# Delta rule levels: one 128x128 block-diagonal tile per matrix instead of two 64x64 tiles, and openings that leave out the next weights

## The chip, the cores and the metric

The kernel runs on one core of one Trainium2 chip. The metric is the time of one execution on the device in microseconds (us).

## The reference, cut to what matters

The program is a transformer of four layers, each an attention part and a feed-forward part, over 8 x 512 rows of 128 numbers in float32. Two of its eight stages hold a delta rule: the attention of layer 0 (here "L0") and that of layer 2 ("L2", with a decay).

```python
A = jnp.where(tri, 0.0, -jnp.einsum('bhncd,bhned->bhnce', kb, k))
for i in range(1, chunk):
    upd = jnp.einsum('...k,...kj->...j', A[..., i, :], A[..., :, :i])
    A = A.at[..., i, :i].add(upd)
inv = A + jnp.eye(chunk, dtype=A.dtype)
u = inv @ v
w = inv @ kb
```

So for each chunk and head a unit triangular matrix is inverted, and its inverse is multiplied with values and keys. The recurrence of L2 is written step by step in the reference; the kernel computes it in chunks as well, with decays in the matrix.

## The kernel before, in words

**Stages and lanes.** The eight stages run one after the other. At each start all compute engines meet: `Run.meet` lets an engine wait for every semaphore that has counted so far. Then the sync engine (SP) issues the DMA that brings the weights of the next stage into the other of two side buffers. A stage's opening clears its buffers on VectorE, the engines meet once more (`run.meet_all()`), and then eight batches are worked off in two lanes, even batches in lane 0 and odd ones in lane 1. Each lane's work is cut into phases, and each engine's instructions are issued in the same order: a phase of lane 0, a phase of lane 1, and so on. An engine works in that order and waits where a semaphore isn't there yet.

**The inverse.** A sequence of 512 steps is four chunks of 128, with four heads. Two chunks are taken together (a pair), which gives 8 matrices of 128x128 (`NT`, the transposed strict part). Each is inverted from its diagonal outwards. First, in level 0, VectorE inverts 2x2 blocks with a few element-wise operations on the four diagonal 32x32 blocks of each matrix (partitions 0 to 31 hold block 0, partitions 32 to 63 block 1, and so on: `part`, `xt` and `x` are 128 x 8 x 32). Levels 1 to 4 join blocks to 4, 8, 16 and 32. Each has a left product (the strict part times the inverse so far, `b[2]`), a mask on VectorE (L899), a right product (L809) with tiles of 32x32, a subtraction (L906) and a 32x32 transpose (L909). Two larger joins follow (L817 to L848), and then the two chunks are applied (L935 and the lines 1089 to 1101 in L0, 2663 to 2675 in L2).

**The left product before.** `strict` is a tile of 128 x 8 x 64. In each half of 64 partitions it holds, for each matrix, a 64x64 tile with two 32x32 blocks on its diagonal; its other half is cleared once at the opening (L791). ScalarE fills it with four copies of 32 partitions (`strict_act`, L856). TensorE multiplies each half with the 64 partitions of `x` in it (L801), so 16 products of 64x64 by 64x32 for each level. VectorE, in `level0_dve`, adds the two 32-column halves of `strict` (L885) to get the diagonal blocks side by side in `part`, masks them (L887), subtracts them from the identity (L889) and transposes (L891).

**Around it.** In L0, TensorE issues after each phase of the first pair a group of six products of a long filter (L1243), and VectorE parts of a short filter (L1258, L1261). In L2, VectorE makes `NT` from the scores and the decays `gt` (L2882), then `AT` (L2885); in L0 ScalarE copies `NT` (L1179) and VectorE masks `AT` (L1316). GpSimd has only the inverse square roots of the norms in these stages (L402, L2948).

Of the kernel before, what the change touches and what calls it, by code (L numbers as in the profile page):

```python
# [7 lines left out]
ALU = mybir.AluOpType  # L8
# [139 lines left out]
                                                  for e in ("PE", "ACT", "DVE", "POOL"))  # L148


class Run:


# [19 lines left out]

    def meet(self, engine):

        for s in self.steps.values():
            if s.count:
                engine.wait_ge(s.sem, s.count)

    def meet_all(self):  # L180
# [571 lines left out]
class Delta:  # L752
# [5 lines left out]
    def __init__(self, c, arena, dv, scaled):  # L758
        self.c, self.dv, self.width = c, dv, HEADS * dv
        self.NT, self.AT, self.X, self.XT, self.T1 = (arena.take(2, HEADS, P) for _ in range(5))  # L760
        small, whole = INVERTED * SMALL, lambda v: v.rearrange("p c h n -> p (c h n)")
        blocks = lambda v, n: v.rearrange("p (m n) -> p m n", n=n)
        self.xt_columns, self.x_columns = whole(self.X)[:, 0:small], whole(self.X)[:, small:2 * small]
        self.xt, self.x = blocks(self.xt_columns, SMALL), blocks(self.x_columns, SMALL)
        self.strict = arena.take(INVERTED, 2 * SMALL)
        self.strict_half = [self.strict[:, :, n * SMALL:(n + 1) * SMALL] for n in range(2)]
        self.part = blocks(whole(self.T1)[:, 0:small], SMALL)
        self.x_half, self.part_half = (blocks(whole(v)[:, 2 * small:], 2 * SMALL) for v in (self.X, self.T1))
        self.NT8, self.XT8 = (v.rearrange("p c h n -> p (c h) n") for v in (self.NT, self.XT))
        self.U = [arena.take(HEADS, dv) for _ in range(2)]  # L770
        self.S, self.gain = arena.take(HEADS * dv), arena.take(HEADS * dv)
        self.own = c(f"blocks{dv}")
        self.carried = arena.take(2, HEADS, dv) if scaled else None
        self.left = self.carried[:, 0] if scaled else arena.take(HEADS, dv)
# [13 lines left out]
    def start_dve(self, dve, u):  # L788

        dve.memset(self.XT, 0.0).then_inc(*u.dve.step())  # L790
        dve.memset(self.strict, 0.0).then_inc(*u.dve.step("strict_cleared"))  # L791

    def levels_pe(self, pe, u, pair, between):
        b = u.banks
        for n in range(1, SMALL_LEVELS):
            pe.wait_ge(*u.dve.at(f"x{pair}_{n - 1}"))
            if n == 1:
                pe.wait_ge(*u.act.at(f"strict{pair}"))
            for m in range(INVERTED):
                for g in map(half_of, range(2)):  # L800
                    made = pe.matmul(b[2][g, m * SMALL:(m + 1) * SMALL], self.strict[g, m, :], self.x[g, m, :])  # L801
            made.then_inc(*u.pe.step(f"left{pair}_{n}"))
            next(between, None)
            yield f"left{pair}_{n}"
            pe.wait_ge(*u.dve.at(f"part{pair}_{n}"))
            half = SMALL // 2
            for m in range(INVERTED):
                for q in map(quarter, range(QUARTERS)):
                    made = pe.matmul(packed(b[3][q, m * half:(m + 1) * half], n), self.part[q, m, :],  # L809
                                     odd_blocks(self.xt[q, m, :], n))  # L810
            made.then_inc(*u.pe.step(f"right{pair}_{n}"))
            next(between, None)
            yield f"right{pair}_{n}"
# [39 lines left out]
    def strict_act(self, act, u, pair):  # L853

        for i in range(QUARTERS):
            act.copy(self.strict_half[i % 2][quarter(i)], self.NT8[quarter(i), :, quarter(i)]).then_inc(*u.act.step(f"strict{pair}"))  # L856

    def levels_act(self, act, u, pair):
        b, half = u.banks, 2 * SMALL
# [22 lines left out]

    def level0_dve(self, dve, u, pair):
        dve.wait_ge(*u.act.at(f"strict{pair}"))
        dve.tensor_tensor(self.part, *self.strict_half, ALU.add).then_inc(*u.dve.step())  # L885
        dve.wait_ge(*u.dve.last())
        dve.tensor_tensor(self.part, self.part, per_tile(self.c("small0"), INVERTED), ALU.mult).then_inc(*u.dve.step())  # L887
        dve.wait_ge(*u.dve.last())
        dve.tensor_tensor(self.xt, per_tile(self.c("small_ident"), INVERTED), self.part, ALU.subtract).then_inc(*u.dve.step())  # L889
# [87 lines left out]
class L0AttnLane:  # L977
    def __init__(self, c, arena, vT, shortT, vearly, vrow):
        self.norm, self.delta = Norm(arena), Delta(c, arena, DK, False)
        self.vT, self.shortT, self.longT = vT, shortT, arena.take(SEQ)  # L980
        self.vearly, self.vrow, self.lrow = vearly, vrow, vearly
        self.before = {name: arena.take(L0_ATTN_CONV - 1 + SEQ) for name in "qkv"}
        self.stat_rows = arena.take(TILES, HEADS, 32)
        self.z, self.zT = arena.take(TILES, P), arena.take(SEQ)
        self.qrow, self.krow, self.vb, self.kb, self.drow, self.kT = (arena.take(TILES, P) for _ in range(6))
# [14 lines left out]
class L0Attn:  # L1000
# [417 lines left out]
    def pool(self, pool, u):  # L1418
# [3 lines left out]
        for phase in ("features", "project", "convolve", "rows", "norms", "keys"):  # L1422
            yield phase
        for pair in range(CHUNKS // 2):
            yield from delta_phases(pair)
        for phase in ["branches", "squares", "lengths", "statistics", "gate", "hidden", "logits", "softmax", "mix",
                      "out", "end"]:
# [1131 lines left out]
class L2AttnLane:  # L2559
    def __init__(self, c, arena):  # L2560
# [5 lines left out]
        self.kbq = arena.take(TILES, 2, P)  # L2566
        self.gt, self.gtm = arena.take(2, HEADS, P), arena.take(2, HEADS, P)
        self.conv = [all_heads(v) for v in (self.gt[:, 0], self.gt[:, 1], self.gtm[:, 0], self.gtm[:, 1])]
        self.steps = [self.a, self.delta.T1[:, 0]]
        self.beta, self.g, self.log = (arena.take(TILES, HEADS) for _ in range(3))  # L2570
        self.low, self.one_more, self.rest = (arena.take(TILES, HEADS) for _ in range(3))
# [8 lines left out]
class L2Attn:  # L2580
# [360 lines left out]
    def pool(self, pool, u):  # L2941
# [10 lines left out]
            yield phase  # L2952
        for pair in range(CHUNKS // 2):
            yield f"between{pair}"
            yield from delta_phases(pair)
        yield "squares"
        yield "roots"
# [916 lines left out]
```

## Time and profile before

| what | value |
|---|---|
| time, median of 3 runs | 5654.37 us (5648.27 to 5659.23) |
| profiled execution, its own time | 5665.99 us |
| its span | 5664.6 us |
| instructions | 93833 |
| TensorE matmul busy | 4062.2 us, 72% |
| TensorE weight load busy | 3146.2 us, 56% |
| VectorE busy | 3020.7 us, 53% |
| ScalarE busy | 1912.0 us, 34% |
| GpSimd busy | 818.4 us, 14% |
| mean granted TensorE clock | 0.76 |

PE is the matmul part of TensorE, PEld its weight loads, DVE is VectorE, ACT is ScalarE, POOL is GpSimd, SPq the queue of SyncE. The granted clock is given as a share of 2.4 GHz: 0.50 is 1.2 GHz. A float32 matmul leaves two records, and so does its weight load; a transpose leaves one. The L0 stage lies between about 17 and 990 us of the span, the L2 stage between about 2844 and 3810 us.

### The profile page before, as it was taken

The page shows a single profiled execution, that of the slowest core. Times are in us where ns is not written, and L with a number is a line of the kernel's source. Part 1 is how long each engine was busy: PE and PEld are TensorE (multiplying, and loading weights), DVE is VectorE, ACT ScalarE, POOL GpSimd, SP SyncE. Part 2 cuts the span into 40 slices and gives each one's busy share as a digit, 9 for nine tenths or more (in the row PEclk, how much of TensorE's full clock was granted, in tenths as well). Part 3 has the DMA queues.
Part 4 walks back from the last instruction along what each step waited for, and adds up shares of the span by engine and source line. Part 5 has one row for each costly group of instructions (what it writes and reads, how often), then busy time and mean ns, then how long its engine had stood idle before and what let it go on. Part 6 is the DMA issues. An engine that isn't in the chain of part 4 may idle for free.

```text
span 5664.6 us, 93833 instructions
## 1 busy us (share of the span) xinstructions
PE 4062.2 (72%) x39179; PEld 3146.2 (56%) x39228; DVE 3020.7 (53%) x8021; ACT 1912.0 (34%) x4196; POOL 818.4 (14%) x600
## 2 busy tenths in 40 slices
PE   6685967568878778773757768577777777776398
PEld 5574846446556555562646557464444555445377
DVE  4445364234554555547255665657666666665333
ACT  2234232123333333330232332325444455552122
POOL 0000000321011101101700000001222111110444
PEclk6555555677898898885756666668888998897599
DMA  9200000330000000001210000000000000000255
GB/s 266 54 2 1 2 1 1 105 113 1 1 1 1 1 1 1 1 1 37 31 41 1 1 1 2 1 2 1 1 1 1 1 1 1 1 1 17 72 164 141
DMA packets 140856, 152.26 MB, mean 27 GB/s; under 512 B 7809, under 2 KB 128003, under 8 KB 139793
## 3 DMA queue, kind: packets, MB, share of 16 engines
q1 hardware_dynamic: 119024, 128.21, 7.7%
q0 software_dynamic: 21408, 18.05, 1.9%
q8 instruction: 309, 5.06, 0.4%
q14 instruction: 115, 0.93, 0.1%
HBM read 87.38 MB, written 59.76 MB: 26 GB/s over the span
## 4 chain that ended last, share of the span: by engine, by line
PE 50%; DVE 29%; ACT 13%; issue 3%; POOL 3%; DMA 2%; SPq 0%; DVEq 0%; POOLq 0%; ACTq 0%
ACT work L3242 4%; PE banks_lane L801 4%; PE banks_lane L422 3%; PE banks_lane L3679 2%; PE banks_lane L1882 2%; PE banks_lane L809 2%; PE banks_lane L3128 2%; PE banks_lane L935 2%; PE banks_lane L3163 1%; ACT work L1976 1%; PE banks_lane L3108 1%; PE banks_lane L3150 1%; POOL room_l_ffn L569 1%; DVE work L2797 1%; DVE weights L3252 1%
## 5 line engine op out<-in xcount | busy, mean ns | idle before, releaser
L422 PE MATMUL banks_lane<-constants,work 128*128 128x128 f32 x968 | 194.4, 346 | 456.2 <-DVE work L408 209.2
L422 PEld LDWEIGHTS banks_lane<-constants,work 128*128 128x128 f32 x968 | 145.3, 178 | 524.9 <-DVE work L408 196.9
L422 PE MATMUL banks_lane<-constants,weights 128*128 128x128 f32 x596 | 126.2, 349 | 349.8 <-DVE weights L408 94.9
L402 POOL TENSOR_TENSOR weights<-weights,constants 128x4 f32<-128x4 f32 x76 | 78.6, 1034 | 1929.6 <-DVE weights L397 1929.6
L422 PEld LDWEIGHTS banks_lane<-constants,weights 128*128 128x128 f32 x596 | 89.3, 180 | 381.6 <-issue 175.0
L3242 ACT ACTIVATE work<-banks_lane,weights 128x192 f32<-128x192 f32 (+1 forms) x512 | 249.3, 505 | 132.5 <-DVE weights L3339 132.5
L402 POOL TENSOR_TENSOR work<-work,constants 128x4 f32<-128x4 f32 x76 | 77.5, 1019 | 1208.8 <-DVE work L397 1208.8
L3346 POOL TENSOR_TENSOR weights<-weights,constants 128x16 f32<-128x16 f32 x64 | 185.5, 2898 | 377.3 <-DVE weights L3254 377.3
L3335 DVE TENSOR_REDUCE weights<-banks_lane 128x2 f32<-128x384 f32 (+1 forms) x256 | 122.4, 520 | 140.2 <-PE banks_lane L3150 140.2
L2029 DVE TENSOR_REDUCE work<-banks_lane 128x2 f32<-128x512 f32 x256 | 158.8, 683 | 67.7 <-PE banks_lane L1896 67.2
L3163 PE MATMUL banks_lane<-constants,work 128*128 128x128 f32 x896 | 135.5, 297 | 80.7 <-DVE work L3327 42.2
L1976 ACT ACTIVATE work<-banks_lane 128x384 f32<-128x384 f32 (+1 forms) x256 | 118.5, 549 | 178.2 <-PE banks_lane L1917 110.0
L3163 PEld LDWEIGHTS banks_lane<-constants,work 128*128 128x128 f32 x896 | 108.1, 152 | 104.5 <-issue 57.0
L3679 PE MATMUL banks_lane<-weights,work 128*128 128x256 f32 x624 | 145.1, 386 | 14.5 <-DVE weights L3721 14.5
L3178 PE MATMUL banks_lane<-work 128*64 128x128 f32 x1792 | 128.1, 288 | 37.2 <-ACT work L3204 37.2
L656 POOL DMA_INDIRECT out<-weights,chunk_places x78 | 121.5, 1558 | 196.5 <-DVE chunk_places L648 130.3
L569 POOL DMA_INDIRECT room_l_ffn<-weights,indices x96 | 92.8, 966 | 362.1 <-DVE weights L392 324.7
L1882 PE MATMUL banks_lane<-weights,work 128*128 128x128 f32 x1024 | 136.7, 298 | 5.9 <-ACT work L1998 5.9
L1882 PEld LDWEIGHTS banks_lane<-weights,work 128*128 128x128 f32 x1024 | 132.7, 213 | 10.3 <-ACT work L1998 10.3
L801 PE MATMUL banks_lane<-work 64*64 64x32 f32 x2048 | 125.1, 292 | 16.5 <-DVE work L891 13.0
L3679 PEld LDWEIGHTS banks_lane<-weights,work 128*128 128x128 f32 x624 | 116.9, 192 | 34.0 <-DVE weights L3721 19.3
L3178 PEld LDWEIGHTS banks_lane<-work 128*64 128x64 f32 x1792 | 100.7, 142 | 62.2 <-ACT work L3204 49.6
(773 smaller groups left out, 10869.7 us busy)
## 6 DMA issues: line engine op xcount, KB each, us to landing
work<-experts_dram_l_ffn SPq DMA_DIRECT2D x39, 964.0 KB, 4.9
room_l_ffn<-work SPq DMA_DIRECT2D x30, 1188.0 KB, 14.7
work<-experts_dram_l_ffn SPq DMA_DIRECT2D x23, 512.0 KB, 3.6
weights<-weights_dram SPq DMA_DIRECT2D x1, 4833.5 KB, 14.3
work<-room_l_ffn SPq DMA_DIRECT2D x36, 132.0 KB, 4.0
weights<-weights_dram SPq DMA_DIRECT2D x1, 4112.0 KB, 13.1
weights<-bands_dram SPq DMA_DIRECT2D x1, 4096.0 KB, 13.1
weights<-room_l_ffn SPq DMA_DIRECT2D x26, 132.0 KB, 4.3
```

The lines of the kernel that those rows point to most:

```text
L402: pool.tensor_tensor(n.rstd, n.rstd, c("neghalf", cols=(0, n.rstd.shape[1])), ALU.pow).then_inc(*u.pool.step(name))
L422: done = pe.transpose(bank[0:rows, t * P:(t + 1) * P], block, c("ident"))
L569: pool.indirect_dma_start(self.room, bass.IndirectOffsetOnAxis(ap=self.where[:, n, t:t + 1], axis=0), rows[n][:, t, :], None).then_inc(*se ...
L801: made = pe.matmul(b[2][g, m * SMALL:(m + 1) * SMALL], self.strict[g, m, :], self.x[g, m, :])
L1882: made = pe.matmul(b[1][:, cols_of(t)], m.ff[:, f, cols_of(t)], self.w(u, f"down{f}"), start=f == 0, stop=f == L1_ATTN_FF - 1)
L1976: act.activation(m.probs[:, hh, 0:blocks, :].rearrange("p b q -> p (b q)"), b[hh][:, 0:blocks * P], ACT.Exp, scale=L1_ATTN_SCALE).then_inc ...
L2029: dve.tensor_reduce(m.top[r][:, :, hh, L1_ATTN_HD], b[hh][:, :].rearrange("p (t c) -> p t c", t=2), AX, ALU.max, negate=True).then_inc(*u. ...
L3163: made = pe.transpose(u.banks[2 + side][:, cols_of(hh)], m.probs[n % 2][:, hh, side * P:(side + 1) * P], self.c("ident"))
L3178: made = pe.matmul(u.banks[2][rows, cols_of(j)], m.v[:, t - 1 + side, at:at + L2_FFN_HD], m.turned[n % 2][:, 4 * side + hh, :], start=side ...
L3242: act.activation(m.probs[n % 2][:, hh, L2_FFN_BACK + lo:2 * P], u.banks[side][:, j * span:(j + 1) * span], ACT.Exp, scale=m.q_factor[:, t, ...
L3346: pool.tensor_tensor(m.rn[:, t, :, :], m.rn[:, t, :, :], c("neghalf", cols=(0, 2 * L2_FFN_HEADS)).rearrange("p (n h) -> p n h", n=2), ALU. ...
L3679: made = pe.matmul(bank[:, g * CHUNK:(g + 1) * CHUNK], self.w(u, f"{name}{f}", cols=(g * P, (g + 1) * P)), m.z[:, f, :], start=f == 0, sto ...
```

## The change

Four things are different.

- The left product takes one 128x128 tile per matrix, with the four 32x32 blocks on its diagonal and zeros elsewhere, and multiplies it with all 128 partitions of `x`: 8 products of 128x128 by 128x32 for each level instead of 16 of 64x64 by 64x32.
- GpSimd makes these tiles: `blocks_pool` multiplies `NT` with a 0/1 mask of diagonal blocks (`blocks32`, a constant), one instruction for each chunk of 128 x 4 x 128. They are stored in buffers that are free at that time: `before["q"]` and `before["k"]` in L0, `gt` in L2. TensorE's first left product waits for them. The 512 columns of the old `strict` tile and its clearing go.
- ScalarE's four copies write to `part`, and the add on VectorE (L885) goes.
- The meeting of the engines leaves out the semaphores of the two weight buffers. The wait for a stage's own weights at its start (`weights_landed`) stays.

```diff
+WEIGHTS = [("DMA", f"weights{n}") for n in range(2)]
...
     def meet(self, engine):
-        for s in self.steps.values():
-            if s.count:
+        for key, s in self.steps.items():
+            if s.count and key not in WEIGHTS:
                 engine.wait_ge(s.sem, s.count)
...
-        self.strict = arena.take(INVERTED, 2 * SMALL)
-        self.strict_half = [self.strict[:, :, n * SMALL:(n + 1) * SMALL] for n in range(2)]
+        self.strict = None
...
     def start_dve(self, dve, u):
         dve.memset(self.XT, 0.0).then_inc(*u.dve.step())
-        dve.memset(self.strict, 0.0).then_inc(*u.dve.step("strict_cleared"))
...
             if n == 1:
-                pe.wait_ge(*u.act.at(f"strict{pair}"))
+                pe.wait_ge(*u.pool.at(f"blocks{pair}"))
             for m in range(INVERTED):
-                for g in map(half_of, range(2)):
-                    made = pe.matmul(b[2][g, m * SMALL:(m + 1) * SMALL], self.strict[g, m, :], self.x[g, m, :])
+                made = pe.matmul(b[2][:, m * SMALL:(m + 1) * SMALL], self.strict[m // HEADS][:, m % HEADS, :], self.x[:, m, :])
...
         for i in range(QUARTERS):
-            act.copy(self.strict_half[i % 2][quarter(i)], self.NT8[quarter(i), :, quarter(i)]).then_inc(*u.act.step(f"strict{pair}"))
+            act.copy(self.part[quarter(i)], self.NT8[quarter(i), :, quarter(i)]).then_inc(*u.act.step(f"strict{pair}"))
+
+    def blocks_pool(self, pool, u, pair):
+        blocks = per_tile(self.c("blocks32"), HEADS)
+        for chunk in range(2):
+            pool.tensor_tensor(self.strict[chunk], self.NT[:, chunk], blocks, ALU.mult).then_inc(*u.pool.step(f"blocks{pair}"))
...
         dve.wait_ge(*u.act.at(f"strict{pair}"))
-        dve.tensor_tensor(self.part, *self.strict_half, ALU.add).then_inc(*u.dve.step())
-        dve.wait_ge(*u.dve.last())
...
+        self.delta.strict = [self.before[name][:, L0_ATTN_CONV - 1:].rearrange("p (h n) -> p h n", n=P) for name in "qk"]
...
         for pair in range(CHUNKS // 2):
+            pool.wait_ge(*u.act.at(f"nt{pair}_{HEADS - 1}"))
+            m.delta.blocks_pool(pool, u, pair)
             yield from delta_phases(pair)
...
+        self.delta.strict = [self.gt[:, 0], self.gt[:, 1]]
...
             yield f"between{pair}"
+            pool.wait_ge(*u.dve.at(f"nt{pair}"))
+            m.delta.blocks_pool(pool, u, pair)
             yield from delta_phases(pair)
```

## Rows read from the trace of the kernel before

**Rows 1.** The page: the span, and each engine's busy time.

```profile
span 5664.6 us, 93833 instructions
...
PE 4062.2 (72%) x39179; PEld 3146.2 (56%) x39228; DVE 3020.7 (53%) x8021; ACT 1912.0 (34%) x4196; POOL 818.4 (14%) x600
```

**Rows 2.** Busy time in stretches: start:end, length, engines, PEclk, DMA share, GB/s.

```profile
574.20:610.00 35.80, 35.80 (x977) 34.11 (x977) 12.76 (x27) 4.93 (x12) 0.00 (x0) 0.50 0.02 4
620.80:636.80 16.00, 16.00 (x79) 15.94 (x78) 3.31 (x10) 1.60 (x6) 0.00 (x0) 0.50 0.00 0
3185.70:3204.00 18.30, 18.19 (x609) 17.62 (x609) 7.47 (x20) 0.81 (x2) 0.00 (x0) 0.50 0.02 4
...
3226.00:3232.00 6.00, 6.00 (x42) 5.58 (x41) 3.34 (x7) 0.74 (x2) 0.00 (x0) 0.98 0.01 3
```

**Rows 3.** Chain of waits in L0, 565 to 640: start, us on it, what.

```profile
574.03 0.76 PE banks_lane L1243 x12
574.79 1.85 PE banks_lane L801 x32
...
577.39 0.98 PE banks_lane L809 x64
...
611.37 1.90 PE banks_lane L841 x16
...
625.70 1.71 PE banks_lane L935 x8
...
628.84 1.55 PE banks_lane L1101 x8
```

**Rows 4.** Chain of waits in L2, 3176 to 3236.

```profile
3185.66 3.62 PE banks_lane L801 x64
3189.28 1.83 PE banks_lane L809 x128
...
3228.47 0.84 PE banks_lane L2675 x8
```

**Rows 5.** TensorE in order of time: first left groups of both lanes, three pairs.

```profile
567.21 1.92 PE L801 MATMUL banks_lane<-weights,work 64*64 64x32 f32 x32
...
572.12 1.92 PE L801 MATMUL banks_lane<-work 64*64 64x32 f32 x32 [0.19 <-DVE work L891]
...
644.13 1.92 PE L801 MATMUL banks_lane<-weights,work 64*64 64x32 f32 x32
...
649.06 1.92 PE L801 MATMUL banks_lane<-work 64*64 64x32 f32 x32 [1.43 <-DVE work L891]
...
3180.79 1.92 PE L801 MATMUL banks_lane<-weights 64*64 64x32 f32 x32 [0.47 <-DVE weights L891]
...
3185.66 1.92 PE L801 MATMUL banks_lane<-work 64*64 64x32 f32 x32 [0.74 <-DVE work L891]
```

**Rows 6.** VectorE, lines 885 and 899: instructions, ns min/median/max, first and last start.

```profile
L885 DVE TENSOR_TENSOR work<-work x24: 424/426/427, 75.6 to 3730.2; 128x256 f32<-128x256 f32 x24
...
L899 DVE TENSOR_TENSOR work<-banks_lane,constants x96: 416/425/426, 81.5 to 3751.2; 128x256 f32<-128x256 f32 x96
```

**Rows 7.** GpSimd by line (busy, mean ns); ScalarE and VectorE in order of time.

```profile
L2080 POOL TENSOR_TENSOR work<-work,weights 128x512 f32<-128x512 f32 x32 | 40.6, 1270 | 0.0
...
644.19 1.20 ACT L1179 COPY work<-banks_lane 128x256 f32<-128x256 f32 x4 [2.16 <-PE banks_lane L782]
...
3180.66 1.38 DVE L2882 TENSOR_TENSOR work<-banks_lane,work 128x256 f32<-128x256 f32 x4
```

**Rows 8.** Waits at two openings: us in total, times, longest.

```profile
DVE work L392 <- DMA weights<-weights_dram: 1.9, 1, 1.9
...
DVE weights L392 <- DMA weights<-weights_dram: 6.7, 1, 6.7
```

**Rows 9.** Chain of waits at the opening of L0.

```profile
21.31 0.48 DVE work L791
```

## The prediction

> **What bounds the kernel now.** I read the page first, for the span and the shares [rows 1], then stretches of the two delta rule stages with their granted clock [rows 2], then the chain of waits through one pair of chunks in each stage [rows 3, 4], and last the matmuls in order of time at the start of a pair [rows 5]. TensorE is busy for 72% of the span, but the share is an average; what counts is the stretch of the levels. There TensorE has no idle time: 35.80 of 35.80 us in the first stage and 18.19 of 18.30 us in the later one, always with a granted clock of 0.50, so 1.2 GHz [rows 2]. The chain says the same: a level of both lanes in L2 is 3.62 us of left products and 1.83 us of right products, back to back, with nothing of VectorE between them [rows 4]. VectorE is busy for a third of that stretch. So in the levels every microsecond of TensorE is one of the span.
>
> **The left products.** Before, a level of a lane has 8 matrices in two halves of 64x64, 16 products. A float32 product leaves two records, so the chain shows 32 records in 1.85 us [rows 3], 0.058 us each. After, it has 8 products of 128x128 on the same 32 columns: 16 records. How long is one? The nearest row is of exactly this shape: L935 multiplies a 128x128 tile by 128x32 float32, 8 records in 1.71 us, 0.214 us each [rows 3]. L1101, the same shape too, has 8 in 1.55 us, 0.194 each [rows 3]. A single 64x64 tile at a time (L841, no second half beside it) has 16 records in 1.90 us, 0.119 each [rows 3]: twice what a record of L801 takes, although its streamed tile is 64 columns wide and L801's is 32. I read this so: the two halves of L801 lie in different rows and columns of the array and work side by side, each at about 0.116 us a record; a 128x128 tile has nothing beside it, and its record is about twice as long as that of a 64x64. Half as many records, each nearly four times as long in the chain, is a loss. A new left group is 16 x 0.214 = 3.42 us; the first L935 group after the 64x64 tiles shows some more, so I take 3.47. Less 1.85 that is +1.62 us a level and lane at 1.2 GHz. Bounds: by L1101 16 x 0.194 = 3.10, +1.25; if each half of the new group took what a whole L801 group takes, plus 0.1 for the change of tile, 3.80, +1.95. I take the row of L935, since it comes in every chunk of the stage and its shape is the same.
>
> The page "TensorEngine Tiling (Array Packing)" of the Trainium skill (Key Properties) says that different tiles of the array run weight loads and matmuls in parallel; the rows of L801 and L841 agree, and by that rule alone the change gives parallel work up. The page "TensorE: Matmul & The Clock Gate" (LDWEIGHTS) puts a weight load at its columns over 1.2 ns; by it, as an estimate, 16 loads of 128 columns would be 1.71 us, a hair less than now, and the sum would have no loss in it. The spacing of L935 is twice that, and the measurement decides.
>
> **How many lie on the path.** Each pair of chunks has four levels, two lanes and so eight left groups; there are 4 pairs of batches x 2 pairs of chunks = 8 such blocks in each stage, 16 in all. Seven groups in each are on the path in full, as TensorE is dense from the first left group of the second lane on [rows 2, 4]. Before that one there is slack [rows 5]. Its start follows from the first lane's group: 3.47, then L899 (0.42 and two hand-overs of 0.02 to 0.04), then in VectorE's order the three operations left of level 0 at 0.46 each (0.43 and the hand-over): 5.35 us after the first lane's start. Before it was 4.93 us (644.13 to 649.06) in the second pair of L0, so +0.4 there. In L2 it was 4.87, and the first lane starts 0.46 earlier, since it waits for a level 0 that is one operation shorter: 0. In the first pair of L0, TensorE itself needs 3.47 + 0.76 + 0.98 + 0.76 = 5.97 with the filter products between, against 4.91: +1.06 [rows 3, 5]. Sum: 16 x 7 x 1.62 = 181.4, plus 4 x 1.06 + 4 x 0.4 = 5.8: **+187 us**. Bounds: 16 x 7 x 1.25 = 140 and 16 x 7 x 1.95 + 10 = 228.
>
> **The add on VectorE.** Level 0 loses L885, 0.43 us [rows 6], 32 times. Its gain is inside the numbers above (three operations instead of four); nowhere else does it show, because TensorE is the bound behind it. The four copies of ScalarE (L856) stay, with another place to write to. At least nothing, at most 32 x 0.46 = 14.7 us, and that only where level 0 ends a wait.
>
> **The blocks on GpSimd.** Two multiplies of 128x512 for each pair and lane, 64 in all. The row for a 128x512 tensor_tensor there is 1.27 us [rows 7], so 2.5 us a pair. In L0 the NT copies end at 645.40 (the ACT row), the blocks at about 648, and the lane's first left group would start at 649.5. In L2 the NT multiplies end at 3182.0, the blocks at 3184.6, and the group starts at 3185.7 [rows 5, 7]. What is queued behind on GpSimd is the square root step of a next batch's norm, a phase of its own that comes after the levels. Cost: 0, hidden behind the copies of ScalarE and level 0 on VectorE with 1.1 to 1.5 us to spare; if the cover went, each us beyond it is one on the path. Both engines read SBUF in that time; where GpSimd works on 128x512 now, it has VectorE beside it, and 1.27 is the mean of 32.
>
> **The openings.** The meeting after the opening memsets waits for the next stage's weights in two stages: VectorE stood 1.9 us at the opening of L1 attention and 6.7 us at that of L2 attention, both released by that DMA [rows 8]. Those go: -8.6 less a normal hand-over of 0.1, so -8.5. Nothing takes their place at the DMA queue: bands are waited for by their own count. The clearing of the old strict tile goes too: 0.48 and its hand-over of 0.06, two lanes, two stages, all on VectorE's chain at an opening [rows 9]: -2.1. Together **-10.6 us**; at least -8, at most -11.
>
> **The sum.** +187 - 10.6 = +176. Against the profiled execution (5665.99 us, of which 5664.6 is the span) that is 5842; against the median of the three runs, 0.2% lower, 5654.4 + 176 = **5830 us**, +3.1%.
>
> **The rivals.**
> *The clock rises in the levels* (ends on the other side). A 128x128 tile fills the array where small tiles did not, and TensorE could be granted 2.4 GHz there. For it: after the 256-column products of L2 the clock goes to 0.98, and a 128x128 group of 8 records takes 0.84 us [rows 2, 4]. Then a left group is 1.68 us, 0.17 less than now, and a right group some 0.49 less: 2 x 0.66 x 4 levels x 16 blocks = -84, with the openings -95: 5560 us. It decides only if about two thirds of the levels run at the high clock, as a block costs +11.3 at the low one and -5.3 at the high one. Against it: the chunk stretch of L0 (620.8 to 636.8) is busy for 16.00 of 16.00 us with 128x128 tiles on 32 and 128 columns and stays at 0.50 [rows 2]; the new groups have that shape. Chance 0.06. A part of it, that the chunk products of L2 behind the levels start at the high clock sooner, would give some 10 to 40 us back and stays inside the range.
> *The new products are as quick as the column rule has it*: 1.71 us a group, so -0.14 x 112 = -16, less the openings and up to 8 us of level 0: about 5622. For it: half the records. Against it: both rows of that very shape. Chance 0.03. The page named above (LDWEIGHTS) is the source of that rule.
> *GpSimd is late*: with two multiplies at 2.5 us each instead of 1.27, it would have the blocks 1.0 to 1.5 us after level 0 in each of the 16 blocks, +20 on top: 5850. It decides from 1.8 us a multiply. For it: an operand of constants read again for each head, and VectorE busy beside it. Against it: the row of 1.27. Chance 0.08.
> *Hidden work, no change*: the levels would have to be bound by VectorE. It is busy for 12.76 of 35.80 us [rows 2]. Chance 0.02.
> *My forecast*, with its own range 5785 to 5870: 0.81.
>
> **How the numbers follow.** The low end is the bound of L1101 with some clock given back: 5654 - 11 + 140 = 5783, less some 15. The high end is the upper bound of the new group with the openings: 5654 - 8 + 228 = 5874. Range 5768 to 5874. A measurement of this kernel tells about 0.2% (11 us) from no change: faster 0.09, within 0.02, slower 0.89.
>
> **What the profile after would show.** Groups of L801 (its new line) with 128x128 tiles, 16 records in about 3.4 us; a level of both lanes in L2 about 8.7 us instead of 5.45; the clock of the level stretches still 0.50; no VectorE wait on weights_dram at the two openings; 64 GpSimd multiplies of about 1.27 us, never the releaser of a left group. The forecast is wrong if the new group takes under 2 us, which a clock over 0.5 in those stretches, or a record well under 0.2 us at 0.5, would show; and its size is off if right products or the stretches behind the levels change clock.

## The result, and the profile after

The kernel after takes 5840.51 us (median of 4 runs, 5838.78 to 5849.59) against 5653.37 us for the kernel before (4 runs on the same chip): a ratio of 1.0334, 95% interval 1.0316 to 1.0352, so 187 us or 3.3% slower. The forecast was 5830 us with a range of 5768 to 5874. The profiled execution has a span of 5838.8 us, 174.2 more than the one of before.

The page of the kernel after, head; it answers to [rows 1]:

```profile
span 5838.8 us, 89808 instructions
...
PE 4274.4 (73%) x37180; PEld 3353.4 (57%) x37180; DVE 3024.5 (52%) x7985; ACT 1910.6 (33%) x4196; POOL 900.0 (15%) x664
```

TensorE has 1,999 matmul records fewer (2,048 by the products; a few are missing from the trace of before) and is busy for 212 us more. VectorE is busy for 4 us more although 36 of its instructions are gone; that is a surprise, explained further down. The 64 multiplies of GpSimd are there (664 instead of 600).

The kernel after in stretches of the levels (first in L0, then in L2) and of the chunk products behind a block in L2; the columns are those of [rows 2]:

```profile
610.40:650.00 39.60, 39.60 (x629) 38.48 (x629) 15.51 (x29) 2.84 (x8) 2.94 (x2) 0.50 0.01 2
3289.60:3316.00 26.40, 26.29 (x481) 25.78 (x480) 6.95 (x18) 0.81 (x2) 0.00 (x0) 0.50 0.01 3
3332.40:3341.80 9.40, 9.40 (x35) 8.60 (x35) 3.04 (x6) 0.74 (x2) 0.00 (x0) 0.50 0.01 2
```

TensorE is still busy without a gap, at 1.2 GHz. The matmuls of the kernel after in order of time, first pair of L0 (start, us, what), against [rows 5]:

```profile
610.44 3.62 PE L801 MATMUL banks_lane<-weights,work 128*128 128x32 f32 x16
613.99 0.83 PE L1248 MATMUL banks_lane<-weights 128*64 128x16 f32 x12
...
616.49 3.62 PE L801 MATMUL banks_lane<-work 128*128 128x32 f32 x16
```

What follows a left group starts 3.55 us after it (613.99 less 610.44); before it was 1.85. And the second lane's first left group starts 6.05 us after the first lane's (616.49 less 610.44), against 4.91 before.

The chain of waits of the kernel after through a block in L2 (start, us on the chain, what), against [rows 4]:

```profile
3286.20 7.04 PE banks_lane L801 x32
3293.23 1.83 PE banks_lane L809 x128
3295.11 7.04 PE banks_lane L801 x32
3302.14 1.83 PE banks_lane L809 x128
...
3332.46 1.90 PE banks_lane L939 x8
...
3338.63 1.71 PE banks_lane L939 x8
...
3343.56 0.93 PE banks_lane L939 x8
```

A level of both lanes takes 8.91 us (3286.20 to 3295.11); the left products are 7.04 of it instead of 3.62, the right ones are unchanged. The chunk products behind the levels begin at the low clock as before and reach the high one later: the third group of L939 (L935 before) is the first at 0.93 us.

The left group's source line in the kernel after (durations in ns, minimum/median/maximum), and what ended the idle time of TensorE ahead of it, its weight loads counted too (us, times):

```profile
L801 PE MATMUL banks_lane<-weights,work x1024: 276/402/423, 78.0 to 3926.8; 128*128 128x32 f32 x171
...
  DVE weights L895: 14.8, 16
  DVE work L895: 6.7, 24
  issue: 2.6, 4
```

The left groups wait for level 0 of VectorE (L895, L891 before), never for GpSimd. What waits for them is VectorE's mask (waits of the kernel after: total us, times, longest):

```profile
DVE work L903 <- PE banks_lane L801: 273.0, 96, 3.9
DVE weights L903 <- PE banks_lane L801: 79.8, 32, 3.0
```

**Stage by stage.** A stage is counted from one DMA of weights that SP issues at a meeting to the next; the first one starts 16.5 to 16.8 us into the span, so a column adds up to the span less that. Each of before and after was profiled twice (the second ones are the last two experiments below), in us:

| stage | before | before again | after | after again | forecast of the difference |
|---|---|---|---|---|---|
| L0 attention | 984.2 | 980.2 | 1078.3 | 1078.3 | +95.5 |
| L1 attention | 1348.7 | 1338.0 | 1331.9 | 1342.0 | -1.9 |
| L2 attention | 969.8 | 969.1 | 1071.2 | 1068.8 | +83.1 |
| the five others | 2345.1 | 2339.1 | 2340.6 | 2337.0 | 0 |

(The forecast per stage: 7 x 8 x 1.62 = 90.7 for each delta rule stage, plus 5.8 in L0, less the opening terms.) The loss lies in the two delta rule stages, +96.1 and +100.5 between the means. L1 attention scatters by 10 us between profiles of the same kernel, so its -16.8 in the first pair of profiles is no effect of the change.

### The profile page after: what moved, and what is told of

The parts are those of the page before. It is cut to its first block and busy times, and to the rows that moved or that the text cites. A ratio compares the mean times of both kernels' runs of the same rounds, so it can differ in the third digit from the quotient of the medians.

```text
span 5838.8 us, 89808 instructions
## 1 busy us (share of the span) xinstructions
PE 4274.4 (73%) x37180; PEld 3353.4 (57%) x37180; DVE 3024.5 (52%) x7985; ACT 1910.6 (33%) x4196; POOL 900.0 (15%) x664
## 5 line engine op out<-in xcount | busy, mean ns | idle before, releaser
L801 PE MATMUL banks_lane<-work 128*128 128x32 f32 x1024 | 231.9, 403 | 4.0 <-DVE work L895 2.7
L801 PE MATMUL banks_lane<-weights,work 128*128 128x32 f32 x1024 | 230.5, 401 | 3.9 <-DVE weights L895 3.8
L801 PEld LDWEIGHTS banks_lane<-weights,work 128*128 128x128 f32 x1024 | 224.3, 332 | 14.0 <-DVE weights L895 11.0
L801 PEld LDWEIGHTS banks_lane<-work 128*128 128x128 f32 x1024 | 223.3, 331 | 9.8 <-DVE work L895 4.0
L862 POOL TENSOR_TENSOR work<-weights,constants 128x512 f32<-128x512 f32 x32 | 40.0, 1271 | 993.0 <-DVE weights L2890 512.4
L903 DVE TENSOR_TENSOR work<-banks_lane,constants 128x256 f32<-128x256 f32 x96 | 40.8, 425 | 273.0 <-PE banks_lane L801 273.0
L871 ACT COPY weights<-weights 32x256 f32<-32x256 f32 x32 | 12.9, 403 | 510.3 <-DVE weights L910 509.9
```

The costliest lines, as they stand in the source:

```text
L801: made = pe.matmul(b[2][:, m * SMALL:(m + 1) * SMALL], self.strict[m // HEADS][:, m % HEADS, :], self.x[:, m, :])
```

## The experiments

Edits are shown against the kernel after where nothing else is said. The first five kernels ask what makes a left group long or short, the next ones what the other parts of the change cost, and the last ones how well a stage's length repeats. In the kernels of the experiments, lines lie one or a few further on: L802 or L801 is the left product, L810 the right one, L1249 or L1248 the filter product.

### The tiles back to 64x64, the rest of the change kept (tiles64)

```diff
-                made = pe.matmul(b[2][:, ...], self.strict[m // HEADS][:, m % HEADS, :], self.x[:, m, :])
+                for g in map(half_of, range(2)):
+                    made = pe.matmul(b[2][g, ...], self.strict[m // HEADS][g, m % HEADS, g], self.x[g, m, :])
```

> The kernel after, but its left products are 16 of 64x64 again, read from the diagonal 64x64 parts of the tiles that GpSimd makes; the openings and level 0 stay as after. Theory (the 128x128 form costs 1.7 us a group, and nothing else costs much): a group is back at 1.85 us; the time is 5654 less 10.6 for the openings, less up to 11 for the shorter level 0, plus some 9 for a VectorE operation slowed by GpSimd, so 5640 us, 5630 to 5655. Rival (GpSimd's tiles or the wait for them carry part of the loss): 5700 or more.

Measured: 5656.02 us, ratio to before 1.0001 (0.9991 to 1.0011). Its matmuls in order of time, first pair of L0:

```profile
570.00 1.92 PE L802 MATMUL banks_lane<-work 64*64 64x32 f32 x32 [0.21 <-DVE work L896]
571.86 0.83 PE L1249 MATMUL banks_lane<-weights 128*64 128x16 f32 x12
572.61 1.92 PE L802 MATMUL banks_lane<-weights,work 64*64 64x32 f32 x32
574.46 0.83 PE L1249 MATMUL banks_lane<-weights 128*64 128x16 f32 x12
```

The group is back at 1.85 us (574.46 less 572.61), and with it 184 us: within the noise, all that the kernel after loses comes from the form of the product. But the rest of the change was to give 10.6 us back and gives nothing: against the runs of before that were measured beside each of them, the openings alone (below) are 11 us faster and this kernel 1.5 us. That leaves some 10 us, each of the two ratios being good to 6 or 7. Something in it costs about as much as the openings bring. A trace of it is the wait of the first lane's first right product for VectorE's mask, 0.84 us, where the kernel before has 0.23:

```profile
567.99 1.05 PE L810 MATMUL banks_lane<-weights,work 32*32 32x16 f32 x64 [0.84 <-DVE work L904]
```

### Full rows, half the columns (cols64), and half the streamed columns (half_columns)

The first cuts each 128x128 product into two of 128 rows by 64 columns; it differs from the one above by keeping the zero rows:

```diff
-                made = pe.matmul(b[2][:, ...], self.strict[m // HEADS][:, m % HEADS, :], self.x[:, m, :])
+                for g in map(half_of, range(2)):
+                    made = pe.matmul(b[2][g, ...], self.strict[m // HEADS][:, m % HEADS, g], self.x[:, m, :])
```

> As tiles64, but each 64-column tile takes all 128 partitions (K = 128, the other 64 are zeros): 16 products of 128x64 by 128x32. Theory (the stationary columns set a record's length, and tiles in different columns work side by side, whatever rows they fill): a group of 32 records in about 2.0 us, as the filter products of 128x64 with their 0.063 us a record, and 5660 us. Rival (the rows have to be free for two tiles to work side by side): 32 x 0.107 = 3.4 us a group and about 5830 us.

The second keeps the 128x128 tile and streams 16 of its 32 columns, so half of the left product is left out:

```diff
-                made = pe.matmul(b[2][:, m * SMALL:(m + 1) * SMALL], ..., self.x[:, m, :])
+                made = pe.matmul(b[2][:, m * SMALL:m * SMALL + 16], ..., self.x[:, m, 0:16])
```

> The kernel after, but each left product streams only 16 of its 32 columns, so half of the left product is left out. Theory (a record of a 128-column tile lasts by its stationary columns, not by what is streamed): a group stays at 3.5 us and the time at 5840 us. Rival (the streamed columns count): 32 to 16 columns take some 13 ns off each of 16 records at 1.2 GHz or more, 0.2 us a group, and 5815 us or less.

Measured: 5659.17 us for the first, 5835.63 us for the second, one run each. A left group of the first in order of time:

```profile
576.04 1.90 PE L802 MATMUL banks_lane<-work 128*64 128x32 f32 x32
577.75 0.81 PE L1249 MATMUL banks_lane<-weights 128*64 128x16 f32 x12
```

and of the second:

```profile
615.92 3.60 PE L801 MATMUL banks_lane<-weights,work 128*128 128x16 f32 x16
619.45 0.83 PE L1248 MATMUL banks_lane<-weights 128*64 128x16 f32 x12
```

1.71 us and 3.53 us. So neither the rows that are filled nor the columns that are streamed, 16 or 32, set the time of these products. (With 64 streamed columns a record of a 128x128 tile is a little longer: 8 in 1.90 us, the row of L939 at 3332.46 above, 0.238 each.) The columns of the stationary tile do, together with whether the other half of the array's columns works meanwhile: 32 records of 64 columns, two side by side, take 1.71 us or 0.053 each; 16 records of 128 columns take 3.55 us or 0.222 each. That is a factor of four for each record, a factor of two for the group. That two tiles work side by side is read from these rates and from L841 in [rows 3], 0.119 us a record for one 64-column tile at a time; a left group with both of its tiles in the same columns was not run.

### 32x32 tiles, read from NT itself (tiles32)

If narrow tiles side by side are good, quarters could be better, and they need no tile of blocks:

```diff
-                pe.wait_ge(*u.pool.at(f"blocks{pair}"))
+                pe.wait_ge(*u.act.at(f"strict{pair}"))
...
-                made = pe.matmul(b[2][:, ...], self.strict[m // HEADS][:, m % HEADS, :], self.x[:, m, :])
+                for q in map(quarter, range(QUARTERS)):
+                    made = pe.matmul(b[2][q, ...], self.NT8[q, m, q], self.x[q, m, :])
...
-            pool.wait_ge(*u.act.at(f"nt{pair}_{HEADS - 1}"))
-            m.delta.blocks_pool(pool, u, pair)
...
-            pool.wait_ge(*u.dve.at(f"nt{pair}"))
-            m.delta.blocks_pool(pool, u, pair)
```

> The opposite direction: the left product of a level as 32 products of 32x32 by 32x32 columns, its stationary tiles read straight from the diagonal of NT. No blocks on GpSimd, no strict tile; the openings, the copies to part and the shorter level 0 stay as after. Theory (four tiles side by side, each record 2 x 32 stationary columns at 1.2 GHz): 64 records in 0.98 us as the right products, 0.87 us less than before for 112 groups on the path, -97, openings -10.6, level 0 -11: about 5535 us, 5520 to 5560. Rival (with 32 streamed columns instead of 16, or with four tiles, a record takes twice that, as the two-tile joins L817 with 0.031): a group of 2.0 us and 5650 us.

Measured: 5689.97 us, ratio 1.0061 (1.0044 to 1.0078): slower than before, and 155 us above what was expected. The groups are as short as hoped, but there are gaps between them. Its matmuls in order of time, in the levels of L0:

```profile
661.59 0.92 PE L810 MATMUL banks_lane<-weights,work 32*32 32x16 f32 x55
664.07 0.31 PE L810 MATMUL banks_lane<-weights,work 32*32 32x16 f32 x9 [1.57 <-issue]
664.21 1.06 PE L802 MATMUL banks_lane<-work 32*32 32x32 f32 x64
665.27 0.96 PE L802 MATMUL banks_lane<-weights 32*32 32x32 f32 x55
667.54 0.33 PE L802 MATMUL banks_lane<-weights 32*32 32x32 f32 x9 [1.31 <-issue]
667.67 1.03 PE L810 MATMUL banks_lane<-work 32*32 32x16 f32 x64
```

TensorE restarts at 664.07 and at 667.54, 3.47 us apart, and in between lie 9 + 64 + 55 = 128 matmul records, with as many weight loads 256 instructions. No semaphore ended these gaps ("issue"). Of the 100 such gaps over 0.3 us in this kernel, 79 come exactly 128 records after the one before. The commonest spacing, 3.45 to 3.49 us, is close to the shortest (3.37); half of the spacings are 3.73 us or more. In the waits of TensorE's matmuls this idle time adds up to 152.7 us, against 13.7 before and none after; its two large lines in this kernel:

```profile
PE banks_lane L810 <- issue: 80.7, 52, 4.2
PE banks_lane L802 <- issue: 56.1, 41, 2.1
```

The reading: TensorE runs out of instructions, which come in batches of 256, one in 3.47 us at best. It was tested next.

### The same with fewer right products (tiles32_half_right)

Against the kernel of the last experiment:

```diff
             half = SMALL // 2
-            for m in range(INVERTED):
+            for m in range(0, INVERTED, 2):
```

> The kernel with 32x32 left tiles, and half of the right products of levels 1 to 4 left out. Theory (in the second pair of each batch TensorE is held by the supply of its instructions, one block of 256 in about 3.4 us, so 512 instructions a level of both lanes take 6.96 us): 384 instructions take 5.2 us a level, and the idle time that only issue explains stays well over 50 us. Rival (the gaps belong to the tiles themselves, a switch of tile or a full queue): the gaps per left group stay, and a level falls by 0.98 us at most, to 6.0.

Measured: 5595.98 us in one run. Its matmuls in order of time:

```profile
634.92 0.76 PE L802 MATMUL banks_lane<-work 32*32 32x32 f32 x41 [1.15 <-issue]
635.48 1.06 PE L802 MATMUL banks_lane<-weights 32*32 32x32 f32 x64
636.34 0.49 PE L810 MATMUL banks_lane<-work 32*32 32x16 f32 x23
638.38 0.31 PE L810 MATMUL banks_lane<-work 32*32 32x16 f32 x9 [1.56 <-issue]
```

With a quarter of the level's matmuls gone, the gaps still come after 41 + 64 + 23 = 128 records, 3.46 us apart. They follow the count of instructions and not the place in the program. In L2, from the start of a block's second level to that of its fourth, a level of both lanes takes 5.23 us in the mean here and 7.02 in the kernel with all right products: 1.5 and 2 batches, expected as 5.2 and 6.96. The rival, no level under 6.0, falls, and 87 us of the idle time stay. So the supply is the bound. A level of the kernel before, with 192 records for both lanes, needs 1.5 batches or 5.2 us as well, and takes 5.49: it stands close above the same bound.

### The meeting alone (openings), twice

Against the kernel before:

```diff
+WEIGHTS = [("DMA", f"weights{n}") for n in range(2)]
...
-        for s in self.steps.values():
-            if s.count:
+        for key, s in self.steps.items():
+            if s.count and key not in WEIGHTS:
                 engine.wait_ge(s.sem, s.count)
```

> The kernel before with one part of the change alone: the meetings leave out the two weight semaphores. Theory: the two waits of 1.9 and 6.7 us at the openings of L1 and L2 attention go and nothing takes their place: 8.5 us less, 5646 us against 5655. Rival (TensorE's granted clock shifts with the start of each stage and takes it back, as the L1 attention stage was 1332 to 1349 us long in the runs so far): anything from 5640 to 5660, with the two waits gone all the same.

Measured: 5641.71 us (12 runs), ratio 0.9983 (0.997 to 0.9995). No wait for the weights' DMA is left in its trace. L2 attention is 962.3 us in both of its profiles (969.8 and 969.1 before); L0 attention is 979.2 and 983.6. A second profile of it, for the scatter of the stages:

> The kernel before with the meeting that leaves out the next weights alone, a second profile. Theory (scatter): layer 1's attention stage between 1331 and 1351 us. Rival (the gain belongs to the meeting): 1331 to 1337 us again, as in the first profile (1335.6). Delta rule stages 979 and 962 us within 5 us.

Measured: 5624.97 us in this one execution; L1 attention 1334.8 us.

### The old meeting in the kernel after (meet_weights)

```diff
-            if s.count and key not in WEIGHTS:
+            if s.count:
                 engine.wait_ge(s.sem, s.count)
```

> The kernel after with the old meetings, which wait for the next weights too. Theory: the waits of 1.9 and 6.7 us are back, 8.5 us more than after, 5849 us. Rival (the clock decides more than the wait): within 5 us of after.

Measured: 5856.55 us in one run, its span 16.4 us above that of after. The waits of VectorE in it:

```profile
DVE weights L395 <- DMA weights<-weights_dram: 7.9, 1, 7.9
DVE work L395 <- DMA weights<-weights_dram: 2.0, 1, 2.0
```

The two waits are back, 9.9 us. L2 attention is 7.6 us longer than after (1078.8); the 7.0 us more in L1 attention are 2.0 of wait and the rest within the scatter of that stage.

### GpSimd's multiplies added to the kernel before (pool_added)

They write to the same free buffers, nobody reads the result, and the first left product waits for them:

```diff
                 pe.wait_ge(*u.act.at(f"strict{pair}"))
+                pe.wait_ge(*u.pool.at(f"blocks{pair}"))
...
+    def blocks_pool(self, pool, u, pair):
+        blocks = per_tile(self.c("blocks32"), HEADS)
+        for chunk in range(2):
+            pool.tensor_tensor(self.spare[chunk], self.NT[:, chunk], blocks, ALU.mult).then_inc(*u.pool.step(f"blocks{pair}"))
```

> The kernel before with GpSimd's 64 multiplies added, into buffers that are free at that time; nobody reads them, but TensorE waits for them at each first left group, as after. Everything else is before. Theory (they slow VectorE operations that read and write SBUF alone: L1258 from 0.74 to 1.35 us, one of the two L2873 from 0.69 to 1.7 us, and TensorE waits behind these): 4 x 0.6 + 8 x 1.0 on the path, about 8 to 20 us more, 5662 to 5675. Rival (the multiplies are hidden, as I forecast): within 5 us of before.

Measured: 5673.88 us, ratio 1.0036 (1.0025 to 1.0047): 21 us slower, without one instruction added to TensorE or VectorE. That is in the expected range, and the rival falls. No wait in its trace is ended by one of these multiplies. Operations of VectorE in it by source line (ns, minimum/median/maximum); the first is L885 of [rows 6], the second L2873:

```profile
L892 DVE TENSOR_TENSOR work<-work x24: 1060/1108/1151, 75.4 to 3753.0; 128x256 f32<-128x256 f32 x24
L892 DVE TENSOR_TENSOR weights<-weights x8: 424/425/427, 2947.9 to 3748.1; 128x256 f32<-128x256 f32 x8
...
L2884 DVE TENSOR_TENSOR work<-constants,weights x16: 677/1218/1758, 2941.2 to 3742.7; 128x512 f32<-128x512 f32 x16
```

The same operations take 0.43 and 0.69 us where GpSimd is idle. In order of time:

```profile
74.95 1.26 POOL L863 TENSOR_TENSOR work<-weights,constants 128x512 f32<-128x512 f32 x1
75.39 1.10 DVE L892 TENSOR_TENSOR work<-work 128x256 f32<-128x256 f32 x1 [0.98 <-ACT work L857]
76.52 0.42 DVE L894 TENSOR_TENSOR work<-work,constants 128x256 f32<-128x256 f32 x1
```

GpSimd's multiply ends at 76.21. Of the 0.82 us that L892 runs beside it, it loses 0.68 (1.10 less 0.42). The next operation, behind the multiply, takes its usual 0.42 us.

Where this reaches TensorE can be read at the start of a block, against the last two lines of [rows 5]:

```profile
3192.17 1.92 PE L802 MATMUL banks_lane<-weights 64*64 64x32 f32 x32 [1.42 <-DVE weights L898]
...
3197.72 1.92 PE L802 MATMUL banks_lane<-work 64*64 64x32 f32 x32 [1.42 <-DVE work L898]
```

The second lane's first left group starts 5.55 us after the first lane's (3197.72 less 3192.17), against 4.87 before: 0.68 more in each of the 8 blocks of L2, or 5.4 us. In L0 the distance is 5.99 us in the first pairs and 5.32 in the second ones, against 4.91 and 4.93: another 5.9 us. With the ways to the next block in L2 (the table further down, 9.8 us more than before) that makes 21 us, the whole of the loss.

### Before and after once more (before_again, after_again)

> The kernel before once more, unchanged, for the stage lengths of a second profile. Theory: the attention stage of layer 1, whose work the change doesn't touch, differs by some us from one profile to the next because the granted clock of TensorE falls otherwise in it; then its length here is anywhere between 1331 and 1351 us, while the two delta rule stages repeat within 5 us (984 and 970 us). Rival: the 16.8 us that this stage lost from before to after belong to the change of the meeting; then it is again 1348 to 1351 us here. Span about 5665 us by the rival, some 5650 to 5665 by the theory.

> The kernel after once more, unchanged, for the stage lengths of a second profile. Theory (scatter of the clock in layer 1's attention stage): that stage is between 1331 and 1351 us, not closely the 1331.9 us of the first profile; the delta rule stages are again 1078 and 1071 us within 5 us. Rival (the stage's gain belongs to the change of the meeting): 1331 to 1336 us again. Span 5835 to 5855 us.

Measured: spans 5643.2 and 5842.6 us. L1 attention is 1338.0 us (1348.7 in the first profile of before) and 1342.0 us (1331.9 in the first of after), so the order of the two is reversed. The delta rule stages stand in the table above: L0 attention of before repeats within 4 us, the others within 2.4. The rival, that L1 attention's 16.8 us belong to the meeting, falls.

## Why the prediction was right

**The bound.** TensorE set the levels before and after, without idle time, as the forecast read it from [rows 2] and [rows 4]; the experiments that changed a left group's time moved the whole by it.

**The left product.** Forecast 3.47 us a group, +1.62; measured 3.55 in L0 and 3.52 in L2 (7.04 for two), +1.70 or +1.71. On 112 groups the 0.08 us are 9 us. The reason given for it holds: a record of a 128x128 tile takes four times what a record of two 64x64 tiles side by side does. cols64 makes it sharper than the forecast had it. "Different rows and columns of the array" isn't the condition; different columns suffice, with all rows filled in both. The rows of L935, of the same shape but in another stretch, were a good price.

The rule of the Trainium skill, "TensorEngine Tiling (Array Packing)" (Key Properties), that tiles of the array work in parallel, agrees with tiles64 and cols64. The one of "TensorE: Matmul & The Clock Gate" (LDWEIGHTS), a load's columns over 1.2 ns, would as an estimate have made a group 1.71 us; it took 3.55, close to what the rows of L935 had given. The same section says that the rows of a weight tile don't count, and cols64 beside tiles64 agrees: 1.71 us with 128 rows, 1.85 with 64.

**The slack of the first groups.** This is the distance from the first lane's first left group to the second lane's, in us; for L2 the forecast is a difference of 0:

| | before | pool_added | after | forecast for after |
|---|---|---|---|---|
| L0, first pair | 4.91 | 5.99 | 6.05 | 5.97 |
| L0, second pair | 4.93 | 5.32 | 5.42 | 5.35 |
| L2, mean of 8 | 4.87 | 5.55 | 5.41 | 4.87 |

In L0 the term came out in size. But pool_added shows nearly the same distances with the short groups, so GpSimd's multiplies alone would have cost as much there; the two causes lie over each other. In L2 the forecast of 0 failed: +0.54 us in each block, 4.3 us in all, where the forecast had level 0 one operation shorter and did not have its first operation 0.68 us longer beside GpSimd.

**L2 attention** is the term that was mis-sized: +83 forecast, +101 and +100 measured. The trace gives it part by part. Each of the 8 blocks is cut at the start of its first left group, the end of its last one, the first and the last chunk product, and the start of the next block. The sums over the stage, in us:

| kernel | levels | joins | chunk products, 1st / 2nd pair | to the next block, in a sequence / to the next sequence |
|---|---|---|---|---|
| before | 189.8 | 96.9 | 85.7 / 76.3 | 46.1 / 346.1 |
| after | 285.9 | 95.7 | 93.4 / 75.9 | 50.4 / 348.0 |
| openings | 188.4 | 96.9 | 87.4 / 75.6 | 46.6 / 345.3 |
| tiles64 | 193.4 | 96.9 | 88.8 / 78.8 | 50.4 / 348.7 |
| pool_added | 194.8 | 96.5 | 85.2 / 77.0 | 52.0 / 350.0 |

The levels take +96.1, 5 more than forecast. Seven groups at +1.71 in eight blocks are 95.8 of it, and the slack above adds 4.3; against that stand some waits that the levels had before and have no more (from the second lane's first left group to its last it was 16.5 to 17.2 us before, and is 26.72 in every block after). The chunk products of the first pairs take +7.7, and the ways to the next blocks +4.3 and +1.9. With -1.6 in the other two and the 6.7 of the opening this is the +101.4 within 0.3.

The +7.7 is the clock. In the block shown above, the stretch of chunk products reaches the high clock 9.4 us after the last join; in the same block before it was 6.0 us. TensorE in order of time in that block of the kernel before:

```profile
3219.92 1.97 PE L935 MATMUL banks_lane<-weights 128*128 128x64 f32 x8
...
3225.94 1.18 PE L935 MATMUL banks_lane<-work 128*128 128x64 f32 x8
```

In the kernel after all four first pairs take 23.3 or 23.4 us and before 21.1 to 21.6. But the second profile of after has one of 20.6 and the second of before one of 23.3, so a few us of it come and go from one execution to the next. Still it goes with the long left groups: in the four profiles of kernels that have them (after twice, meet_weights, half_columns) 15 of 16 first pairs take 23.3 or 23.4 us, in the four of before and openings 2 of 16. What makes the rise come later is not shown. The forecast had this stretch the other way, as a possible gain of 10 to 40 us.

The ways to the next blocks are GpSimd's. They are longer by much the same, 4 to 6 us and 2 to 4 us in tiles64 and pool_added, which have its multiplies, and not in openings, which has not.

**GpSimd** is the step whose reason was wrong. The forecast put its cost at nothing, because the blocks are ready in time, and they are: no left group waits for them, the multiply takes 1.27 us in the median (forecast 1.27), and the rival "GpSimd is late" falls. But it asked only when GpSimd is done, not what it does to VectorE meanwhile, although it named that both read SBUF then. In pool_added, with the work of TensorE and VectorE otherwise untouched, it costs 21 us; tiles64 stands some 10 us above openings. The kernel after pays part of it too. VectorE's operations by source line in the kernel after:

```profile
L2881 DVE TENSOR_TENSOR work<-constants,weights x16: 678/1218/1759, 3006.0 to 3890.0; 128x512 f32<-128x512 f32 x16
...
L1263 DVE TENSOR_SCALAR weights<-weights x4: 1350/1351/1352, 79.8 to 878.4; 128x1024 f32<-128x1024 f32 x4
```

and the same in the kernel before:

```profile
L2873 DVE TENSOR_TENSOR work<-constants,weights x16: 681/689/694, 2934.5 to 3720.4; 128x512 f32<-128x512 f32 x16
...
L1258 DVE TENSOR_SCALAR weights<-weights x4: 742/744/744, 80.9 to 810.1; 128x1024 f32<-128x1024 f32 x4
```

In L2 the kernel after loses 6.2 us to it between the blocks, by the table above, and at most the 4.3 us of the slack. In L0 it isn't told apart from the longer group: no kernel was run in which another engine makes the 128x128 tiles.

**The openings.** Forecast -10.6 us: -8.5 for the waits and -2.1 for the clearing. openings gives the first alone as 11.2 us by the medians (5652.87 less 5641.71; by the interval of the ratio between 3 and 17), and L2 attention is 7.1 us shorter in it. The waits themselves were 1.9 and 6.7 us. The clearing shows in L0: GpSimd starts the first norm's root at 28.73 us instead of 29.74, 1.0 us sooner, where the forecast has 1.05. In L2 no gain is seen: from the stage's start to its first left group it is 91.0 and 91.6 us in the two profiles of after, and 90.8 and 90.9 in those of openings, which still clears.

**The sum.** Forecast +176 us. Measured +174.2 between the first two profiles, +199 between the second two, and +187 between the medians. The closeness of the first is luck in part: a gain of 16.8 us in L1 attention, which is scatter, stood against a loss in L2 that the forecast had 17 to 18 us too small. By the two delta rule stages alone it is +196.6 against a forecast of +178.6, 9% short.

**The clock** stayed at 0.50 in the levels, and the rivals in which it rises, in which the work is hidden, or in which a group takes 1.71 us fall with the rows of the kernel after.

## What to carry to other kernels

At 1.2 GHz, small float32 products (16 or 32 streamed columns) were priced by the columns of their stationary tile and by how many column groups of the array work side by side, not by rows filled or columns streamed: a bigger tile with zeros in it halves the records and doubled the time of a group (1.85 to 3.55 us) where TensorE was the bound. Going the other way has a floor of its own: at 256 instructions in 3.47 us at best, 32x32 tiles were starved, so count a level's instructions as well as its time. And work put on an idle engine isn't free just because it is ready in time: GpSimd's multiplies, late for nobody, cost 21 us through VectorE; the part of this change worth keeping is the meeting that leaves out the next weights (0.9983 of before).

## What the runs showed that was not expected

**VectorE nearly stands while GpSimd multiplies.** A VectorE operation on 256 or 512 columns with both operands in SBUF loses about four fifths of the time that it overlaps with a two-operand multiply of GpSimd. L892 lost 0.68 of 0.82 us. (One on 128 columns, L1336 in L0, lost half: 0.34 of 0.68.) In order of time in the kernel after:

```profile
3271.41 2.48 POOL L862 TENSOR_TENSOR work<-weights,constants 128x512 f32<-128x512 f32 x2 [57.96 <-DVE weights L2890]
3272.69 2.36 DVE L2881 TENSOR_TENSOR work<-constants,weights 128x512 f32<-128x512 f32 x2
```

GpSimd ends at 3273.89, so they overlap for 1.20 us; the two operations take 2.36 instead of 2 x 0.69 = 1.38 and lose 0.98. L1263, whose one tensor is in SBUF, goes from 0.74 to 1.35 us, and there GpSimd pays as well: the multiply that begins while L1263 still runs takes 1.72 us instead of 1.27. The operations that read one operand from PSUM (L2893, L1321, L903) keep their 0.42 us beside it. In the lines above GpSimd's own two multiplies take 2.48 us for both, no more than without VectorE beside them. The Trainium skill, "VectorE: DVE Perf Modes" (Two Vector instructions with no wait between them), speaks in passing of a second SBUF read interface that VectorE shares with GpSimd, for a second SBUF tensor or the one input of a 2-port mode; that operations with two tensors in SBUF are slowed and those with one in PSUM are not agrees with that. Whether L1263 runs in such a mode no run here shows, and the size of the loss is from the runs.

**TensorE's instructions come in batches of 256**, one in 3.45 to 3.49 us at best, in tiles32 and tiles32_half_right alike. By the page of the profile, the DMA queue q8, called instruction, moves 341 packets and 5.59 MB in tiles32, 309 and 5.06 MB before, and 293 packets after. The differences are TensorE's: tiles32 has 4,096 matmuls and as many loads more than before, which is 32 x 256, and 32 packets more; after has 2,048 and 2,048 less, which is 16 x 256, and 16 packets less. So a packet of 16,384 bytes is 256 instructions. The times of the packets in the traces say the same: each of the 100 restarts in tiles32 comes 1.19 to 1.60 us after a packet of q8 has ended, and each of the 64 in tiles32_half_right 1.22 to 1.58 us. So TensorE's supply is this queue. What sets its 3.47 us is not shown. The kernel before stops in this way 8 times, for 13.7 us with the shorter gaps, and the kernel after never.
